# Keeping v with 17 columns a head, storing it once a chunk from SyncE, and nine slots for the loaded heads

## What is computed

```python
allowed = (j % 4 == 0) | (jnp.abs(i - j) <= 8)       # i: query row, j: key row
q = (xn @ q_w), k = (xn @ k_w), v = (xn @ v_w)       # each split into 16 heads of 16 features
q = q * jax.nn.sigmoid(unity_scale)
scores = jnp.einsum('bhqd,bhkd->bhqk', q, k) / jnp.sqrt(D)
attn = jax.nn.softmax(jnp.where(allowed, scores, -jnp.inf), axis=-1)
out = jnp.einsum('bhqk,bhkd->bhqd', attn, v)         # heads joined again, then:
x = x + (out @ o_w + o_b) + (fp8(xn) @ w_dq.T + bias)
```

## Time and profile before

| | |
|---|---|
| median of 3 runs | 1153.3 us (1152.36 to 1155.88) |
| profiled execution, its own time | 1152.31 us |
| its span, first to last instruction | 1150.5 us |
| busy: PE, DVE, ACT, POOL | 1079.3, 943.4, 807.8, 249.7 us |
| DMA packets | 192506, 150.74 MB |
| queue of SyncE (q1) | 125.32 MB, 35.4% of 16 engines |
| queue of ScalarE (q10) | 23.66 MB, 7.5% |

### The profile page before, as it was taken

One profiled execution on the slowest core, in us unless ns is written; L12 is line 12 of the kernel. 1 busy time (PEld: TensorE's weight loads), 2 busy tenths in 40 slices (PEclk: granted clock), 3 DMA queues, 4 the chain that ended last, 5 costly groups with the idle time before them and its releaser, 6 DMA issues.

```text
span 1150.5 us, 28768 instructions
## 1 busy us (share of the span) xinstructions
PE 1079.3 (94%) x10944; PEld 491.8 (43%) x10944; DVE 943.4 (82%) x1203; ACT 807.8 (70%) x1524; POOL 249.7 (22%) x381
## 2 busy tenths in 40 slices
PE   5899999958999999999999999999999999999896
PEld 3566555623333333333333334333333333333485
DVE  5887767558999999999999999999999999998032
ACT  2444333316888888888888888888888888888500
POOL 1433333310221222122121212222121212212100
PEclk9999999976999999999999999999999999999998
DMA  6677777763323333333333333333333333232267
GB/s 188 181 216 218 226 214 232 215 195 97 91 84 112 95 101 91 109 97 94 98 106 99 93 96 112 95 95 97 109 95 92 95 109 102 84 113 81 95 239 283
DMA packets 192506, 150.74 MB, mean 131 GB/s; under 512 B 35628, under 2 KB 171564, under 8 KB 192364
## 3 DMA queue, kind: packets, MB, share of 16 engines
q1 hardware_dynamic: 154632, 125.32, 35.4%
q10 hardware_dynamic: 37744, 23.66, 7.5%
HBM read 79.86 MB, written 67.77 MB: 128 GB/s over the span
## 4 chain that ended last, share of the span: by engine, by line
PE 64%; DVE 11%; SPq 11%; issue 8%; DMA 3%; ACT 1%; ACTq 1%; DVEq 0%
PE ps_attend L1145 16%; PE ps_attend L1075 12%; SPq L255 10%; PE ps_attend L1110 9%; DVE peak_far L1017 9%; PE ps_attend L1152 6%; PE ps_attend L1085 4%; PE ps_attend L1225 4%; PE ps_attend L1121 3%; PE ps_attend L1088 3%; PE ps_attend L1128 2%; PE ps_project L605 1%; PE ps_project L595 1%; DMA heads<-attn_dram 1%; PE ps_project L574 1%
## 5 line engine op out<-in xcount | busy, mean ns | idle before, releaser
L1017 DVE TENSOR_REDUCE peak_far<-ps_attend 128x2 f32<-128x1024 f32 x512 | 608.8, 1221 | 46.9 <-PE ps_attend L1110 42.6
L947 ACT ACTIVATE probs<-ps_attend 128x512 f32<-128x512 f32 x1024 | 539.2, 598 | 46.9 <-PE ps_attend L1075 43.8
L1145 PE MATMUL ps_attend<-probs,v_op 128*32 128x512 f32 x2048 | 273.1, 606 | 0.0
L1075 PE MATMUL ps_attend<-q_op,k_op 51*128 51x512 f16 x1024 | 259.8, 386 | 5.9 <-ACT probs L947 3.3
L1110 PE MATMUL ps_attend<-k_op,q_op 48*128 48x512 f16 x1024 | 185.8, 388 | 24.7 <-DVE peak_far L1017 15.4
L952 ACT ACTIVATE probs<-ps_attend 108x512 f32<-108x512 f32 x256 | 139.0, 594 | 37.4 <-PE ps_attend L1088 37.4
L1075 PEld LDWEIGHTS ps_attend<-q_op,k_op 51*128 51x128 f16 x1024 | 78.0, 93 | 201.3 <-ACT probs L947 137.5
L809 POOL CAST negmax<-peak 128x16 bf16<-128x16 f32 x64 | 12.7, 198 | 627.8 <-DVE peak L1000 627.8
L1020 DVE TENSOR_REDUCE peak_near<-ps_attend 128x8 f32<-128x864 f32 x128 | 131.0, 1023 | 11.2 <-PE ps_attend L1128 11.1
L800 POOL TENSOR_TENSOR out_rows<-out_rows,share_rows 128x512 f32<-128x512 f32 x64 | 81.4, 1272 | 49.2 <-DMA share_rows<-shares_dram 46.5
L1110 PEld LDWEIGHTS ps_attend<-k_op,q_op 48*128 48x128 f16 x1024 | 49.8, 94 | 95.7 <-DVE peak_far L1017 69.2
(11 more groups left out here) (80 smaller groups left out, 1039.8 us busy)
## 6 DMA issues: line engine op xcount, KB each, us to landing
v_dram<-v_sb ACTq DMA_DIRECT2D x64, 256.0 KB, 6.3
share_rows<-shares_dram SPq DMA_DIRECT2D x64, 256.0 KB
attn_dram<-out_rows SPq DMA_DIRECT2D x64, 256.0 KB, 5.6
v_op<-v_dram SPq DMA_DIRECT2D x48, 288.0 KB
q_dram<-qk_parts SPq DMA_DIRECT2D x96, 128.0 KB
k_dram<-qk_parts SPq DMA_DIRECT2D x96, 128.0 KB
q_op<-q_dram SPq DMA_DIRECT2D x128, 96.0 KB, 2.4
k_op<-k_dram SPq DMA_DIRECT2D x64, 144.0 KB, 3.1
```

The source lines that it names most:

```text
L947: ins = nc.scalar.activation(probs[:, r, h], ps_s[st.bank(kind)], ACT.Exp, scale=undo)
L1017: ins = nc.vector.tensor_reduce(peak_far[:, :, p, tile], banks, AX_X, ALU.max)
L1075: nc.tensor.matmul(bank, k[half(f, KM), keys], q[half(f, KM), p], start=True, stop=True).then_inc(s_ready, 1)
L1145: ins = nc.tensor.matmul(ps_o[h * VW:(h + 1) * VW], v[:, r, h * VW:(h + 1) * VW], probs[:, r, h], start=(r == 0), stop=False)
```

## The change

v and its ones are kept with 17 columns a head (`VR = D + 1`: 16 of v and a single 1.0) in `v_sb`, `v_dram` and `v_op`. `v_dram` is laid out by sequence with all 16 heads in a row, so a chunk is stored with one transfer of 544 KB (pieces of 1088 bytes) where there were four of 256 KB (pieces of 512 bytes). SyncE issues it, between k high and k low, where it now also waits for ScalarE's copy. A load of v into `v_op` has pieces of 272 bytes where there were 512. In `weigh` a head's stationary operand is 17 columns wide and its result 17 rows; one matmul before the first step's `weigh` gives the unused rows of that PSUM bank a value. `heads` has nine slots. SyncE loads the first nine chunks within the steps, one each in steps 17, 21, 25, ..., 49, at the end of the step's work; ScalarE loads the last seven after the steps, each when the projection of the chunk nine before it is done. The output projection's loops are written out.

The diff, cut to its core:

```diff
+VR = D + 1
+HEADS = 9
@@ part_project
-        v_sb = sb("v_sb", [P, 2, TT, NH, VW])
+        v_sb = sb("v_sb", [P, 2, TT, NH, VR])
@@ sync_project, body
-                for w, part in ((0, HI), (0, LO), (1, HI), (1, LO)):
+                for w, part in ((0, HI), (0, LO), (1, HI), (None, None), (1, LO)):
+                    if w is None:
+                        sp.wait_ge(v_copied, c + 1)
+                        row = LOCAL + cq * CH
+                        sp.dma_start(dram["v"][bass.ds(j + n // CPB, 1), row:row + CH, :].rearrange(
+                            "b (t p) w -> p (b t) w", p=P), v_sb[:, k].rearrange("p t h w -> p t (h w)")
+                            ).then_inc(v_stored[k], 16)
+                        continue
@@ scalar_project, body
-                        act.wait_ge(v_stored[k], 16 * TT * earlier(j, n))
+                        act.wait_ge(v_stored[k], 16 * earlier(j, n))
...
-                    act.wait_ge(v_copied, c + 1)
-                    b4, cq = (j + n // CPB) * G, n % CPB
-                    for t in range(TT):
-                        row = LOCAL + cq * CH + t * P
-                        act.dma_start(dram["v"][bass.ds(b4, G), row:row + P, :].rearrange("g p w -> p g w"),
-                                      v_sb[:, k, t].rearrange("p (g h) w -> p g (h w)", g=G)).then_inc(v_stored[k], 16)
@@ part_attend
+    def fetch_heads(eng, b, n):
+
+        for k in range(OUTS):
+            eng.wait_ge(attn_stored[k], 16 * len(range(k, ((b + 1) * G - 1) * CPB + n + 1, OUTS)))
+        for i in range(KC):
+            load_heads(eng, b, n, i)
@@ sync_attend, load_v
-            v = dram["v"][it]
+            v = dram["v"][it // G, :, it % G * HG * VR:(it % G + 1) * HG * VR]
@@ sync_attend, body
-            elif st.at(3) < STEPS + CPB:
-                if st.at(3) == STEPS:
-                    for k in range(OUTS):
-                        sp.wait_ge(attn_stored[k], 16 * len(range(k, G * CPB, OUTS)))
-                for i in range(KC):
-                    load_heads(sp, 0, st.slot(3), i)
...
             if ("negmax",) in st.entries():
                 move_negmax(st)
+            if G * CPB <= st.n < G * CPB + HEADS * CPB and st.n % CPB == 1:
+                fetch_heads(sp, st.n // (G * CPB) - 1, st.n // CPB % CPB)
@@ scalar_attend
-        with act.Fori(1, B - 1) as j:
-            for n in range(CPB):
-                act.wait_ge(y_ready, CPB * j + n - CPB + 1)
-                for i in range(KC):
-                    load_heads(act, j, n, i)
...
+        for c in range(HEADS, B * CPB):
+            act.wait_ge(y_ready, c - HEADS + 1)
+            fetch_heads(act, c // CPB, c % CPB)
@@ tensor_attend, weigh
+                else:
+                    nc.tensor.matmul(ps_o, keep["ident_bf"][:], mask_k[:, 0:CH], start=True, stop=True)
...
-                    ins = nc.tensor.matmul(ps_o[h * VW:(h + 1) * VW], v[:, r, h * VW:(h + 1) * VW], probs[:, r, h],
+                    ins = nc.tensor.matmul(ps_o[h * VW:h * VW + VR], v[:, r, h * VR:(h + 1) * VR], probs[:, r, h],
```

More of the change, by code:

```diff
@@ L192, in part_project @@
         spare = keep["base"].rearrange("p t f -> p (t f)")[:, (B - 1) * S // P * H:]
-        zeros = spare[0:NIT, -LOCAL * HG * VW // 2:]
+        zeros = spare[0:B, -LOCAL * NH * VR // 2:]
         def earlier(j, n):
@@ L754, in part_attend @@
     attn_stored = [sem(f"attn_stored{i}") for i in range(OUTS)]
-    heads_loaded = [sem(f"heads_loaded{i}") for i in range(CPB)]
+    heads_loaded = [sem(f"heads_loaded{i}") for i in range(HEADS)]
     y_ready = sem("y_ready")
@@ L759, in part_attend @@
     out_stored = sem("out_stored")
-    heads = keep["heads"]
+    heads = sb("heads", [P, HEADS, KC, CH])
     ps_y = [ps[:, 2 * i:2 * i + 2] for i in range(CPB)]
@@ L909, in sync_attend @@
             sp.wait_ge(done["qk_stored"][k], 16 * 12 * B * CPB // 2)
-            sp.wait_ge(done["v_stored"][k], 16 * TT * B * CPB // 2)
+            sp.wait_ge(done["v_stored"][k], 16 * B * CPB // 2)
         load_v(0, 0)
@@ L966, in scalar_attend @@
                     act.wait_ge(done["qk_stored"][k], 16 * 12 * B * CPB // 2)
-                    act.wait_ge(done["v_stored"][k], 16 * TT * B * CPB // 2)
+                    act.wait_ge(done["v_stored"][k], 16 * B * CPB // 2)
             body(Step(0, n))
-        for k in range(OUTS):
-            act.wait_ge(attn_stored[k], 16 * len(range(k, (B - 1) * G * CPB, OUTS)))
-        with act.Fori(1, B - 1) as j:
-            for n in range(CPB):
-                act.wait_ge(y_ready, CPB * j + n - CPB + 1)
-                for i in range(KC):
-                    load_heads(act, j, n, i)
[L976 to L982, removed]
+        for c in range(HEADS, B * CPB):
+            act.wait_ge(y_ready, c - HEADS + 1)
+            fetch_heads(act, c // CPB, c % CPB)
     def vector_attend(dve):
@@ L1211, in body, with project @@
             far_unit(0, 1)
-        def project(j, n):
-            c = CPB * j + n
-            pe.wait_ge(heads_loaded[n], 16 * KC * (j + 1))
-            if not (isinstance(c, int) and c < CPB):
-                pe.wait_ge(total_ready, c - CPB + 1)
+        def project(b, n):
+            c = b * CPB + n
+            pe.wait_ge(heads_loaded[c % HEADS], 16 * KC * (c // HEADS + 1))
+            if b >= 1:
+                pe.wait_ge(total_ready, (b - 1) * CPB + n + 1)
             elif n == 0:
@@ L1238, in tensor_attend @@
             body(Step(0, n))
-        for n in range(CPB):
-            project(0, n)
-        with pe.Fori(1, B - 1) as j:
-            for n in range(CPB):
-                project(j, n)
-        for n in range(CPB - 1):
-            project(B - 1, n)
-        pe.wait_ge(heads_loaded[CPB - 1], 16 * KC * B)
+        for c in range(B * CPB - 1):
+            project(c // CPB, c % CPB)
+        pe.wait_ge(heads_loaded[(B * CPB - 1) % HEADS], 16 * KC * ((B * CPB - 1) // HEADS + 1))
         for t in range(TT):
@@ L1249, in tensor_attend @@
             for i in range(KC):
-                last = nc.tensor.matmul(last_y[t][:, 0:H], heads[:, CPB - 1, i, t * P:(t + 1) * P],
+                last = nc.tensor.matmul(last_y[t][:, 0:H], heads[:, (B * CPB - 1) % HEADS, i, t * P:(t + 1) * P],
                                         keep["wo"][:, i], start=(i == 0), stop=(i == KC - 1))
@@ L1280, in build @@
             "undo": sb("undo", [P, 1]),
-            "heads": sb("heads", [P, CPB, KC, CH]),
             "peak_far": sb("peak_far", [P, 2, PAIRS, TT]),
```

24 lines of the change are left out of this document (12 added, 12 removed).

## The result

| | before | after |
|---|---|---|
| median, us | 1153.64 (1152.36 to 1155.88, 4 runs) | 1127.26 (1125.79 to 1128.99, 4 runs) |
| ratio | | 0.977, 95% interval 0.9749 to 0.9791 |
| profiled execution, its own time | 1152.31 | 1128.99 |
| span | 1150.5 | 1127.2 |
| busy: PE, DVE, ACT, POOL | 1079.3, 943.4, 807.8, 249.7 | 1070.1, 948.4, 811.9, 248.4 |

The changed kernel is 26.4 us faster; the forecast was 1129.8. Two of its terms were sized wrong and one stood at nothing where there was a loss, and these errors nearly cancel. The two profiled executions differ by less, 23.3 us, because that of before is the fastest of its four runs and that of after the slowest. I split these 23.3 at two events: up to the first matmul of the attention -17.0; from there to the first matmul of the output projection +1.3; from there to the end -7.7 (rounding leaves 0.1).

What follows compares the result with a forecast made beforehand. SyncE's queue, slowed by traffic, was taken to pace the later projections; TensorE paces the steps. 1152.3 - 16.5 (handover) - 2.0 (`weigh`) - 5.0 (end) = 1128.8, or 1129.8 us at the median; likeliest 1126 to 1132, wider range 1123 to 1142.

Steps and rivals of the forecast that it cites:

- The v stores, the chunks: Projections: with 2.65 MB a chunk, chunks 8 to 15 run at 12.94 us, chunk 15 beginning 8.4 us earlier.
- Rival B: Projections: SyncE's time is issue time, so one more transfer makes its chunk 15.0 us; 1162 us, 5 in 100.
- rival A: Projections: half the relief, SyncE's issues stay stretched by its v store, 13.5 us a chunk; about 1139, 18 in 100.
- The handover: Projections to attention: q high no longer waits, attention starts at 227.6 instead of 244.13; 16.5 us, including the chunks' 8.4.
- v in smaller pieces: Loads of v in the steps: 272-byte pieces cost nothing, as the last load has 13 us until its use.
- rival F: Loads of v: pieces under 512 B make the first `weigh` wait; 1145 us at 14 us a load, 2 in 100.
- `weigh`: Steps: 17-column weight loads take 96 ns instead of 109, saving 0 to 4.1 us, taken as 2.
- Heads in the steps: Nine steps: extra loads on SyncE's queue behind the maxima's transfer cost 0, with 10 us as far end.
- Rival C: Nine steps: loads of heads disturb the maxima by up to 1.1 us each; 1140 us, 4 in 100.
- The end: Output projection: TensorE ends 1.4 us earlier and output stores catch up; 5.0 us less, 6.6 if the last store takes 3.
- Rival D: Output projection: output stores stay backed up and only TensorE's 1.4 us come; 1133 us, 10 in 100.

Runs made afterwards that it cites:

- the two corner kernels: Changed kernel with 32 columns a head, one 1 MB v store a chunk: 1144.88 us; kernel before with 17 columns alone, four v stores: 1130.11 us.
- the second series: Changed kernel timed again, beside the one loading heads in two halves: 1127.31 us, ratio 0.9784.
- the halves: Changed kernel with each 512 KB load of heads cut into two 256 KB transfers, two steps apart: 1121.98 us, and 1123.08 us when repeated.

## Why the prediction was right, and where it was not

**The v stores, the chunks: right.** Forecast: chunks of 12.94 and chunk 15 at 217.0; the trace has 12.94 and 216.75. I had argued that either bytes or pieces would come out under the pace; the two corner kernels show that it is the bytes. 3.15 MB a chunk don't keep up with 2560 pieces either (222 GB/s), and 2.65 MB keep up in 4096. SyncE's new issue takes 0.40 us where I took 1.0, at the low end of my bounds; nothing depended on it. Six q stores take 4.75 us, where I had named about 4 as a sign. Rival B (SyncE's issue time is the bound) is refuted by chunks of 12.94 us with one transfer more in SyncE's queue, and rival A (half the relief) by the full cadence.

**The handover: right, 0.4 us short.** Forecast 227.6, found 227.17; -17.0 where I said -16.5. q high waits for TensorE alone.

**v in smaller pieces: right, rival F is out.** No `weigh` waits for a v load. Even stores in pieces of 272 bytes kept the pace of 12.94. The Trainium skill, "DMA: Bandwidth & Descriptors", Specifications, asks for pieces of at least 512 B; of that the runs show the busy share of 0.74 instead of 0.66, and no time.

**`weigh`: the mechanism right, the term undersized.** The load takes 95 ns (forecast 96), but I took half of the 4.1 us because VectorE or ScalarE might set the step. The step shortened by 0.06 us, 3.8 us in all, and wide loads alone bring it back to 12.68: TensorE sets the step. 0.06 us over five rounds is 12 ns a round, about what one load got shorter; that one load a round is exposed fits this, and no run shows it by itself.

**Heads in the steps: wrong.** "I take 0" was the failed step, and so was its reason, "they stand behind the maxima's transfer, not ahead". The maxima were indeed untouched. But the queue has a second small transfer with little room, the sums, a step's turn later. The sign I had named, longer steps at the nine that load heads, came. I priced the loads against the one transfer for which the trace of before had a wait in the steps, and not against the others that come after them. In the profiled execution the long steps add 5.6 us (2.0 in that of the second series); over the series the halves show 4.2. Rival C named the wrong transfer for this order of the queue. With the heads ahead of the maxima it names the right one, but its 1.1 us a step falls short of the up to 3.3 measured.

**The end: right in kind, undersized.** TensorE ends 1.7 us earlier relative to its start (forecast 1.4). The last stores take 2.5 us to land (median of four) where I took 4.6 from a queue that was still backed up, so the span ends 3.4 us after TensorE instead of 5.7. -7.7 in place of -5.0; my far end was 6.6. Rival D (nothing but TensorE's part) is out.

**The sum.** Between the first attention matmul and the output projection the execution of after has -3.8 us for the weight loads, +5.6 for the late sums, -0.7 for a long step that only before had (13.33), and the stretch before the regular steps. For that, the windows of after, from the first attention matmul to the first maxima's transfer and on to the second:

```profile
227.17:243.65 16.48, 9.72 (x64) 4.23 (x63) 14.88 (x15) 1.29 (x2) 0.83 (x4) 0.69 0.31 99
243.65:260.06 16.41, 12.87 (x82) 4.44 (x81) 11.94 (x12) 8.94 (x16) 0.83 (x4) 0.50 0.33 75
```

Before, these were 17.47 and 15.54 us at a mean granted clock of 0.60 and 0.53. So the first is 1.0 shorter and the second 0.9 longer, as its clock was granted: at half speed (1.2 GHz) throughout, since the half-clock stretch from 237.0 to 260.9 covers it. The next interval is 0.26 longer. The added matmul (0.6 us at that clock) is in the second. No run took it out; its share of the 0.9 is not shown. In sum: -3.8 + 5.6 - 0.7 - 1.0 + 0.9 + 0.3 = +1.3. Against my terms the errors are -0.5 (handover), -1.8 (weight loads), +5.6 (sums), -2.7 (end), and -0.5 for the rest of this paragraph: +0.1 in all. That the sum came within 0.2 us of this execution (1128.8 against 1128.99) is luck: it rests on a loss of 5.6 that I had at nothing and on 5.5 of gains beyond my terms. That it came within 2.5 of the median is partly so.

**Open.** Why a chunk's traffic stops at 222 GB/s (231 in one window, from 40 to 92 us of the kernel with one store of 1024 KB) while 357 are reached at the end is not settled: the busy share of the DMA engines is only 0.70 to 0.76 there. It is an average, too: from 191 to 204 us the kernel before moved 246 GB/s at a busy share of 0.82. The mix of stores and loads differs, and no run separated the two.

## What to carry to other kernels

When traffic on a shared queue sets the pace, count the bytes of a stage against its wanted length first: here a stage that needed 205 GB/s kept up in each of the forms and from each of the queues tried, and one that needed 243 did not in either form tried (it got 222 over most of the stage). Before adding a large transfer to a queue, list every small transfer that follows it until the queue is empty, also those a step later and those whose issue waits for a landing; each has its own room, and the room of one says nothing about the next. Splitting the large transfer over two steps took away the loss that none of the three places tried in the step avoided: with the halves the medians of the two series are 1122.0 and 1123.1 us, the best of all.

## What was unexpected of the hardware

- With 512 KB queued ahead of it, an 8 KB store releases the next issue after 5.0 to 5.9 us (median 5.3), with 256 KB after 3.1 to 4.7 (3.6), and with neither after 1.8 to 4.2 (3.0), while the DMA engines are busy for some 0.3 of the time (the page's slices in the steps).
- v stores in pieces of 272 bytes were part of a stage that moved 201 GB/s at a busy share of 0.74; with v in pieces of 1088 bytes it was 205 GB/s at 0.66.
- A 128 KB store at the end lands in 2.5 us after (DMA busy share 0.42 from 1121 to 1124 us) and in 4.6 before, where the stores were backed up (1.02 from 1141 to 1146).
- A wait of 2.55 us on TensorE was followed by 3.4 us at the lower level of its clock, and the step with it took 16.4 us where those without took at most 14.8.
